# Four cross attentions, one self attention and a routed expert stage of a decoder on one Trainium2 core: first queries copied directly, first maxima placed by a table, rows of maxima moved in the queue, routed counts summed by TensorE

## The chip, the cores and the metric

One program runs on 1 core of one Trainium2 chip. The metric is the device time in microseconds (us), the median of the runs. The engines are TensorE (PE, its weight loads PEld), VectorE (DVE), ScalarE (ACT), GpSimd (POOL) and SyncE (SP), which issues most DMAs. SBUF holds the tiles, PSUM (`ps`) the products of TensorE.

## What is computed

The reference takes x (16, 112, 256) and a context (16, 375, 256), and adds to x, layer by layer, a gated attention and a gated feed-forward part, each on the normalised rows of x:

```
x = x + tanh(g_xattn[0]) * cross_attention_0(LN(x), ctx)
x = x + tanh(g_ffn[0])   * experts_by_position(LN(x))
x = x + tanh(g_xattn[1]) * cross_attention_1(LN(x), ctx)
x = x + tanh(g_ffn[1])   * lora_experts(LN(x))
x = x + tanh(g_xattn[2]) * decoder_block(LN(x), ctx)   # self attention, cross attention, relu layers
x = x + tanh(g_ffn[2])   * product_keys(LN(x))
x = x + tanh(g_xattn[3]) * cross_attention_3(LN(x), ctx, masks)
x = x + tanh(g_ffn[3])   * routed_top2_experts(LN(x))
```

A cross attention has 16 heads of 16 dimensions: q = x Wq + bq, k and v from the context, softmax(q k^T * scale) v, then Wo. The routed layer takes, for each of 16*112 rows, the two best of 8 experts; each expert is a gated layer of 1024 with a normalisation of its own.

## The kernel before

The program is a chain of stages (`chain()`, from L3245). Each stage gives one program to each engine, and `stage` (L182) ends it with a meeting: every engine drains, adds one to a semaphore and waits for all five. The order of the work on each engine is written out by hand; SP's order of DMAs is the order of its one hardware queue. In the profile these stages begin at about: context 0 us, cross 0 at 309, cross 1 at 671, queries of the self attention at 1229, self attention at 1276, cross 2 at 1430, cross 3 at 2177, routed experts at 2438; between them lie the experts by position, the LoRA experts, and the relu and product-key stages.

The context stage makes keys and values of all four cross attentions for all 16 batches and stores them in DRAM (`key_parts`, `values`). So that bf16 products give nearly float32 scores, a float32 number is held as three bf16 parts (high, middle, low: `PARTS` = 3), and six products of parts are summed in one matmul of 96 rows: `Q_PART` = (0, 0, 0, 1, 1, 2) says which part of the queries stands in each sixth of the rows (`spread(j)`, every sixth row), `K_PART` the same of the keys. Two more rows (96 and 97) hold the negative maximum of each query, in two bf16 parts, against rows of ones in the keys.

**A cross stage** (`cross_stage`, L943) treats 16 batches; four batches are a group (`G` = 4 groups, 448 query columns each).
- Queries (`Queries`, L656). TensorE projects (L689): per group two tiles of 128 dimensions, each with two matmuls of 448 columns. ACT makes the high part (L705), DVE the remainder (L719), ACT the middle part (L700), POOL the low part (L729). SP stores each tile with its three parts in DRAM (`query_parts`, `store`, L676), waits until it has landed, and loads it again as six DMAs in the layout of the score matmuls (`load_queries`, L1011). The weights Wq and Wo and two bias rows are loaded by SP at the beginning of the stage (L651, L653), but for cross 0, whose loads end the context stage.
- Maxima. For each batch 8 `pair`s (L1113): two heads' scores, 112 x 375 each, in two of four PSUM banks; DVE takes the negative maxima of a pair (L1269, with masks L1265). After the eighth, DVE clamps (L1278, L1276), TensorE transposes (`maxima`, L1119), DVE splits the row in two parts (L1284, L1286), and SP copies them into rows 96 and 97 of the batch's queries (`rows`, L1021, two DMAs of 3.5 KB). Their arrival is counted in the same semaphore as the batch's values (`at_maxrow`, `load_values`, L1016).
- A `step` of a batch has 12 score tiles (L1129, with a mask matmul L1126 in cross 3), which ACT exponentiates (L1235), and 48 small products with the values (`weigh`, L1139). Between the score tiles of batch b stand the 8 pairs of batch b + 2 (`PAIR_AT`), the transposition of the maxima of b + 1 at k = 2, and the output of b - 1 (L875, L881, L887). All 16 pairs of batches 0 and 1 stand ahead of step 0.

SP's order at the beginning of a cross stage: weights; keys of batch 0 and 1 (six DMAs each, L931; in cross 3 keys of 0 and three masks); store group 0 and wait for it; load its queries; store 1; keys of 2; stores 2 and 3; values of 0; rows of 0; values of 1 and 2; wait for the stores; queries of group 1. In step b: keys of b + 3, rows of b + 1, values of b + 3.

```
1150      q.project(pe)
1151      for b in range(2):
1152          arrived(b, b, turn0)
1153          for p in range(PAIRS):
1154              pair(b, b, p)
1155          if b == 0:
1156              maxima(0, 0)
```

**Self attention.** `query_stage` projects queries and keys (4 tiles a group, weights loaded at its beginning), with the same stores (L676) and reloads for group 0 (L755, L761); it ends when all stores have landed. `self_stage` loads the other groups.

**Routed experts** (`routed_experts_stage`, L2795). Router logits (L943), the two best experts (L1792 to L1807), then both one-hots are added (L3114) and counted: two float32 matmuls, with a lower triangle (L3009, rows ahead in the batch) and with ones (L3010, rows of the batch). DVE adds the counts of the 16 batches one after another (L3121, 16 instructions), derives the blocks of each expert, adds them one after another (L3126, 7 instructions), and finds the expert of each of 21 blocks (L3127 to L3130), by which POOL gathers the weights (L2926). Then each row's place among the blocks: for each of the two choices compares with 43 bounds (L3146), a sum (L3148), a one-hot of the lane, 112 x 2048 (L3150), and three planes of a one-hot of the block (L3153, L3154, L3155). TensorE inverts the table (L3014, 32 matmuls), DVE turns it into indices (L3167 to L3174), and POOL gathers the rows (L2940), which TensorE turns and multiplies (L3039, the main loop). POOL splits the first weights (L2961) before it gathers rows.

## Time and profile before

| | us |
|---|---|
| median of 3 runs | 2940.99 (2938.33 to 2943.34) |
| the profiled execution, its own time | 2937.35 |
| its span, first to last instruction | 2935.6 |
| TensorE busy in the span | 2572.4 (88%), granted clock 0.919 on the mean |
| DVE, ACT, POOL busy | 1801.1 (61%), 1346.3 (46%), 1127.6 (38%) |
| DMA | 361.72 MB, mean 123 GB/s |

Busy time of an engine is a share of the span; the granted clock is a share of 2.4 GHz, with 0.50 and 1.00 its two levels. A stage in which TensorE is busy less than the others shows where it waits; the views by stretch and by time, quoted below, show for whom.

### The profile page before, as it was taken

The page shows a single profiled execution, that of the slowest core. Times are in us where ns is not written, and L with a number is a line of the kernel's source. Part 1 is how long each engine was busy: PE and PEld are TensorE (multiplying, and loading weights), DVE is VectorE, ACT ScalarE, POOL GpSimd, SP SyncE. Part 2 cuts the span into 40 slices and gives each one's busy share as a digit, 9 for nine tenths or more (in the row PEclk, how much of TensorE's full clock was granted, in tenths as well). Part 3 has the DMA queues.
Part 4 walks back from the last instruction along what each step waited for, and adds up shares of the span by engine and source line. Part 5 has one row for each costly group of instructions (what it writes and reads, how often), then busy time and mean ns, then how long its engine had stood idle before and what let it go on. Part 6 is the DMA issues. An engine that isn't in the chain of part 4 may idle for free. (4 is left out here: it accounts for less than half of the span.)

```text
span 2935.6 us, 57244 instructions
## 1 busy us (share of the span) xinstructions
PE 2572.4 (88%) x21432; PEld 2096.7 (71%) x21432; DVE 1801.1 (61%) x3917; ACT 1346.3 (46%) x2698; POOL 1127.6 (38%) x1409
## 2 busy tenths in 40 slices
PE   7999799997997999869699898888868994999995
PEld 7999487883876777636377666666746873999995
DVE  5666587125874343368488437787758874566765
ACT  4454366323663111247466433344433661555663
POOL 3444311003113333247612233554362113677773
PEclk9999699996998999979799999889977995999998
DMA  8888855327550000062466300000027733455663
GB/s 230 243 246 242 235 160 153 119 88 188 164 174 15 1 0 1 31 165 65 121 185 167 119 1 1 1 1 1 1 69 201 181 95 128 189 203 202 214 221 110
DMA packets 153628, 361.72 MB, mean 123 GB/s; under 512 B 26496, under 2 KB 110336, under 8 KB 138160
## 3 DMA queue, kind: packets, MB, share of 16 engines
q1 hardware_dynamic: 141632, 273.03, 33.0%
q0 software_dynamic: 11760, 85.51, 8.2%
q8 instruction: 152, 2.49, 0.4%
q14 instruction: 84, 0.69, 0.1%
HBM read 269.33 MB, written 88.67 MB: 122 GB/s over the span
## 5 line engine op out<-in xcount | busy, mean ns | idle before, releaser
L1235 ACT ACTIVATE arena<-ps 125x448 f32<-125x448 f32 x768 | 404.7, 545 | 325.9 <-PE ps L1129 321.9
L1269 DVE TENSOR_REDUCE arena<-ps 112x2 f32<-112x750 f32 x384 | 348.4, 931 | 82.2 <-PE ps L1113 79.3
L502 POOL TENSOR_SCALAR ln_var<-ln_mv 112x1 f32<-112x1 f32 x160 | 43.0, 269 | 768.1 <-DVE ln_mv L496 763.8
L3039 PE MATMUL ps<-moe_x_r,moe_w_r 128*128 128x256 f32 x2016 | 254.8, 288 | 9.2 <-DVE arena L3199 7.8
L1129 PEld LDWEIGHTS ps<-arena,wreg 98*125 98x125 bf16 x2304 | 215.8, 143 | 60.6 <-issue 18.9
L3039 PEld LDWEIGHTS ps<-moe_x_r,moe_w_r 128*128 128x128 f32 x2016 | 249.1, 195 | 12.0 <-DVE arena L3199 8.8
L1113 PE MATMUL ps<-wreg,arena 96*112 96x375 bf16 x768 | 217.7, 372 | 31.9 <-DMA arena<-query_parts 18.6
L1129 PE MATMUL ps<-arena,wreg 98*125 98x112 bf16 x2304 | 237.3, 228 | 3.7 <-ACT arena L1235 2.9
L1139 PE MATMUL ps<-arena 125*17 125x112 f32 x6144 | 199.2, 263 | 0.6 <-ACT arena L1235 0.6
L428 POOL TENSOR_TENSOR arena<-arena 128x375 bf16<-128x375 f32 x128 | 114.6, 918 | 166.4 <-ACT arena L365 166.4
L285 PE MATMUL ps<-kv_ctx_r,kv_w_r 128*128 128x376 f32 x768 | 145.7, 339 | 21.5 <-DVE kv_w_r L391 14.6
L3084 ACT ACTIVATE arena<-ps,wreg 128x256 f32<-128x256 f32 x168 | 80.1, 477 | 171.4 <-PE ps L3039 152.7
L2961 POOL TENSOR_TENSOR moe_w_r<-wreg,moe_w_r 128x512 fp32r<-128x512 f32 x105 | 139.5, 1355 | 39.7 <-ACT moe_w_r L3067 39.3
L1139 PEld LDWEIGHTS ps<-arena 125*17 125x17 f32 x6144 | 133.4, 98 | 28.6 <-issue 10.8
L285 PE MATMUL ps<-kv_w_r,kv_ctx_r 128*125 128x256 f32 x1152 | 149.5, 282 | 0.0
L3050 PE MATMUL ps<-wreg,arena 128*128 128x256 f32 x672 | 148.5, 380 | 0.0
L285 PEld LDWEIGHTS ps<-kv_ctx_r,kv_w_r 128*128 128x128 f32 x768 | 130.9, 190 | 24.7 <-issue 22.1
L2611 POOL TENSOR_TENSOR arena<-arena 112x1024 f32<-112x1024 f32 x48 | 90.6, 1905 | 149.6 <-DVE arena L2730 138.7
L1265 DVE CUSTOM_DVE_ANT_0 ps<-ps,arena 112x375 f32<-112x375 f32 x256 | 134.2, 573 | 20.0 <-PE ps L1113 17.9
L285 PEld LDWEIGHTS ps<-kv_w_r,kv_ctx_r 128*125 128x125 f32 x1152 | 144.8, 186 | 0.0
L3050 PEld LDWEIGHTS ps<-wreg,arena 128*128 128x128 f32 x672 | 126.4, 191 | 16.0
L399 DVE SCALAR_TENSOR_TENSOR arena<-ps,attn_cols,arena 128x375 f32<-128x375 f32 x128 | 71.9, 604 | 104.1 <-ACT arena L361 103.9
(363 smaller groups left out, 5879.4 us busy)
## 6 DMA issues: line engine op xcount, KB each, us to landing
wreg<-key_parts SPq DMA_DIRECT2D x288, 187.5 KB, 4.0
key_parts<-arena SPq DMA_DIRECT2D x128, 281.2 KB, 4.0
arena<-query_parts SPq DMA_DIRECT2D x108, 224.0 KB, 4.6
values<-arena SPq DMA_DIRECT2D x64, 357.0 KB
arena<-values SPq DMA_DIRECT2D x64, 357.0 KB
arena<-key_parts SPq DMA_DIRECT2D x96, 187.5 KB, 4.0
query_parts<-arena SPq DMA_DIRECT2D x40, 336.0 KB, 5.7
wreg<-in_e_w SPq DMA_DIRECT2D x16, 704.0 KB, 5.3
```

Source lines behind the costliest of these rows:

```text
L285: mm = pe.matmul(dst, lhs(i, c), rhs(j, c), start=(n == 0 and c == 0), stop=(n == len(PRODUCTS) - 1 and c == DC - 1))
L428: pool.tensor_tensor(parts[i % 2][:, t, 2, :], rest[i % 2][:, t, :], parts[i % 2][:, t, 1, :], ALU.subtract).then_inc(part_lo, 1)
L1113: mm = pe.matmul(ps[0:T, 2 * (p % 2) + e, 0:S2], queries(b)[0:SROWS, hd, :], keys[r][0:SROWS, hd, :], start=True, stop=True)
L1129: mm = pe.matmul(ps[0:KN, bank, g * T:(g + 1) * T], keys[r][:, hd, c * KN:(c + 1) * KN], queries(b)[:, hd, :], start=not masked, stop=not ...
L1139: mm = pe.matmul(ps[32 * g:32 * g + VW, SUMS, j * T:(j + 1) * T], vals[r][:, c, 4 * j + g, :], probs[(j * KC + c) % PROBS][:, g * T:(g + 1 ...
L1235: act.activation(probs[k % PROBS], ps[0:KN, 4 + k % 2, 0:GT], ACT.Exp, scale=scale).then_inc(at_probs, 1)
L1265: mm = dve.tensor_tensor_reduce(bank, bank, pen[r], 1.0, 3 * NEG, ALU.add, ALU.max, negmax[r % 2][:, 2 * p + e:2 * p + e + 1])
L1269: dve.tensor_reduce(negmax[r % 2][:, 2 * p:2 * p + 2], ps[0:T, 2 * (p % 2):2 * (p % 2) + 2, 0:S2], AX.X, ALU.max, negate=True).then_inc(at ...
L2611: pool.tensor_tensor(sums[hd], sims[q][:, hd, 0:PI].unsqueeze(2).broadcast_to([T, PI, PK]), sims[q][:, PH + hd, :].unsqueeze(1).broadcast_ ...
L2961: pool.tensor_tensor(w_r[1][:, :, :, cols], w_in[j % 2][:, :, :, cols], w_r[0][:, :, :, cols].bitcast(F32), ALU.subtract).then_inc(m_low, 1)
L3039: mm = pe.matmul(ps[:, f % 4, q * BS:(q + 1) * BS], w_r[wp][:, q, c, f * 128:(f + 1) * 128], x_r[u][xp][:, c, :], start=(n == 0 and c == 0 ...
L3050: mm = pe.matmul(ps[:, 5 + u, q * D:(q + 1) * D], hid[u][:, f, q * 128:(q + 1) * 128], w_out[u][:, f, :], start=(f == 0), stop=(f == FC - 1))
```

## The change

- `Queries.spread_first`: the parts of group 0 are copied from SBUF straight to the layout of the scores, each level as soon as both its tiles are made; no store and no reload of group 0, in the four cross stages (queries) and in the query stage (queries and keys). Columns of Wq are permuted on the host (`by_halves`) so that a partition of the parts holds both tiles of two neighbouring heads; `query_parts` gets rows of 1,792 B. The parts lie as (part, tile), and a store is one DMA per group and kind.
- `QueryWeights` are loaded in the stage before: in the context stage ahead of its last stores, at the beginning of the experts by position, during the self attention, in the product-key stage (Wo of cross 3 in the stage itself). One bias row instead of two, one DMA for each weight.
- A table (`FIRST_PAIRS`, `MAXIMA_AT`): only batch 0's pairs and two of batch 1 stand ahead of step 0; step 0 holds 12 pairs (6 of batch 1, 6 of batch 2), step 1 holds 10 (2 of batch 2, 8 of batch 3). From step 2 on it is as before. The projection of group 3 is cut in four and laid between the pairs of batch 0 (`LAST_GROUP_AT`).
- SP: keys of 0, direct queries, keys of 1, stores 1 and 2, values of 0, rows of 0, keys of 2, values of 1; in step 0 keys of 3, rows of 1, then queries of group 1, values of 2, store of group 3, values of 3. The rows have a semaphore of their own.
- POOL fills each key tile's rows of ones between the low parts of two groups, no longer all behind.
- Routed experts: one-hots, triangle and ones in bf16; the matmul with ones comes first; the counts of earlier batches are added by 15 further matmuls in PSUM; DVE sums over batches in one reduction (`of_expert`) and over experts by a product with a table (`blocks_ahead`) and a reduction. Block and lane come from a rounding (`WHOLE`) for both choices at once; the block's one-hot is one comparison, its second plane DVE's, its first ACT's. Two planes instead of three. POOL waits for the row indices only, not for those of the way back.

```diff
+            def spread_first(self, sp, kind, dest, order, arrived):
+                for level, made in enumerate((part_hi, part_mid, part_lo)):
+                    sp.wait_ge(made, self.q0 + (kind + 1) * DC)
+                    for j, q in enumerate(order):
+                        if q == level:
+                            sp.dma_start(dest[spread(j), :, :].rearrange("d h n -> d (h n)"),
+                                         self.parts[0][:, q, kind * DC:(kind + 1) * DC, :].rearrange("p t n -> p (t n)")).then_inc(arrived, 16)
...
+        LAST_GROUP_AT = {1: (0, 0), 3: (0, 1), 5: (1, 0), 7: (1, 1)}
+        FIRST_PAIRS = ({0: ((1, 2), (1, 3)), 1: ((1, 4),), 2: ((1, 5),), 3: ((1, 6),), 4: ((1, 7),), 6: ((2, 0),), 7: ((2, 1),),
+                        8: ((2, 2),), 9: ((2, 3),), 10: ((2, 4),), 11: ((2, 5),)},
+                       {0: ((2, 6),), 1: ((2, 7),), 3: ((3, 0),), 4: ((3, 1),), 5: ((3, 2),), 6: ((3, 3),), 7: ((3, 4),), 8: ((3, 5),),
+                        9: ((3, 6),), 10: ((3, 7),)})
+        MAXIMA_AT = (6, 3)
...
                 load_keys(sp, keys[0], kv, 0, 0)
-                q.store(sp, 0)
-                q.stored(sp, 0)
-                load_queries(0, range(len(Q_PART)))
-                q.store(sp, 1)
...
+                q.spread_first(sp, 0, group_q[0], Q_PART, group_in[0])
+                weights.load_late(sp)
+                load_keys(sp, keys[1], kv, 1, 1)
+                for g in range(1, G - 1):
+                    q.store(sp, g)
                 load_values(0, 0)
-                rows(0, 0)
+                rows(0)
+                load_keys(sp, keys[2], kv, 2, 2)
+                load_values(1, 1)
...
                     if has(b, 1):
-                        rows(b + 1, place(1))
+                        rows(b + 1)
+                    if b == 0:
+                        q.stored(sp, G - 2)
+                        load_queries(1, range(len(Q_PART)))
+                        load_values(2, 2)
+                        q.store(sp, G - 1, q_last)
...
+                pe.wait_ge(loaded, q.ready)
+                q.project(pe, range(G - 1))
+                arrived(0, 0, turn0)
+                for p in range(PAIRS):
+                    pair(0, 0, p)
+                    if p in LAST_GROUP_AT:
+                        tile, chunk = LAST_GROUP_AT[p]
+                        q.project_tile(pe, G - 1, tile, (chunk,))
+                arrived(1, 1, turn0)
+                pair(1, 1, 0)
+                maxima(0, 0)
+                pair(1, 1, 1)
...
+                    pe.wait_ge(row_in, row_in0 + (n0 + b + 1) * 32)
...
                 for p in range(PAIRS):
                     reduce_pair(0, 0, p)
                 clamp(0, 0)
                 split_rows(0, 0)
+                q.remainders(dve, range(G - 1, G))
...
-                for b in range(B):
-                    link(dve.tensor_tensor(run[:, b + 1, :], run[:, b, :], counts[:, b, :], ALU.add))
+                link(dve.tensor_reduce(of_expert, ps[:, 2, 0:B * E].rearrange("p (b e) -> p e b", e=E), AX.X, ALU.add))
...
-                for e in range(1, E):
-                    link(dve.tensor_tensor(first[:, e:e + 1], first[:, e - 1:e], blocks_of[:, e - 1:e], ALU.add))
+                link(dve.tensor_tensor(blocks_ahead, ahead, blocks_of.unsqueeze(1).broadcast_to([128, E, E]), ALU.mult))
+                link(dve.tensor_reduce(first, blocks_ahead, AX.X, ALU.add))
...
-                pool.wait_ge(m_inverse, INVERTED)
+                pool.wait_ge(m_inverse, INVERTED - 4)
```

## Rows read from the trace of the kernel before

**Rows 1.** Busy time by stretch: us; busy of each engine; PEclk, DMA share, GB/s.

```profile
372.00:500.00 128.00, 125.54 (x2030) 102.55 (x2029) 107.80 (x189) 87.29 (x187) 20.25 (x47) 1.00 0.63 176
671.00:716.00 45.00, 29.19 (x68) 12.04 (x69) 19.89 (x28) 10.45 (x18) 22.47 (x18) 0.65 0.80 223
...
2438.00:2497.00 59.00, 18.50 (x106) 17.25 (x107) 32.54 (x86) 6.57 (x12) 23.37 (x64) 0.50 0.44 161
2497.00:2890.00 393.00, 385.24 (x2663) 367.61 (x2663) 254.72 (x498) 226.97 (x502) 286.46 (x274) 0.99 0.56 197
```

**Rows 2.** Who waited for whom, whole trace, PE: us in total, times, longest us.

```profile
PE ps L689 <- DMA attn_rows<-in_attn_rows: 35.8, 5, 8.1
...
PE ps L1113 <- DMA arena<-query_parts: 18.6, 8, 5.9
```

**Rows 3.** Instructions in order of time, cross 1, from its first DMA on.

```profile
670.71 0.39 SPq L651 DMA_DIRECT2D wlow<-in_attn_w  x1
...
677.91 9.20 PE L689 MATMUL ps<-xn_t,wlow 128*128 128x448 f32 x16 [7.65 <-DMA attn_rows<-in_attn_rows]
...
685.20 2.03 POOL L729 TENSOR_TENSOR arena<-wreg,arena 128x448 bf16<-128x448 f32 x2 [9.32 <-ACT arena L700]
...
700.62 7.51 DVE L1269 TENSOR_REDUCE arena<-ps 112x2 f32<-112x750 f32 x8 [5.44 <-PE ps L1113]
...
709.37 1.17 SPq L1021 DMA_DIRECT2D arena<-arena  x2
...
715.74 0.62 PE L1129 MATMUL ps<-arena,wreg 98*125 98x112 bf16 x4
```

**Rows 4.** DMA issues of cross 0's beginning, 309 to 360 us: KB each, median us to landing.

```profile
DMA packets 5447, 12.11 MB, mean 237 GB/s; under 512 B 949, under 2 KB 4277, under 8 KB 4869
...
arena<-query_parts SPq DMA_DIRECT2D x12, 224.0 KB, 4.7
```

**Rows 5.** In order of time: first instruction of cross 0, 2 and 3; batch 3's transposition in each cross.

```profile
309.66 5.13 POOL L1070 MEMSET wreg<- 2x3000 f32 x2 [4.36 <-SPq L192]
...
374.18 0.26 PE L1119 MATMUL ps<-ident,arena 112*16 112x112 f32 x1
...
739.81 0.26 PE L1119 MATMUL ps<-ident,arena 112*16 112x112 f32 x1
...
1430.30 0.39 SPq L651 DMA_DIRECT2D wlow<-in_attn_w  x1
...
1497.93 0.26 PE L1119 MATMUL ps<-ident,arena 112*16 112x112 f32 x1
...
2177.16 0.39 SPq L651 DMA_DIRECT2D wlow<-in_attn_w  x1
...
2254.33 0.26 PE L1119 MATMUL ps<-ident,arena 112*16 112x112 f32 x1
```

**Rows 6.** Cross 3, in order of time: two pairs; SP's rows of batch 1; step 1's beginning.

```profile
2210.21 1.89 PE L1113 MATMUL ps<-wreg,arena 96*112 96x375 bf16 x4 [0.20 <-DVE arena L1265]
...
2226.20 1.17 SPq L1021 DMA_DIRECT2D arena<-arena  x2
...
2236.88 0.63 PE L1126 MATMUL ps<-unit,arena 112*125 112x448 bf16 x1 [1.81 <-DMA arena<-arena]
```

**Rows 7.** Who SP waited for, 1262 to 1280 us, the end of the query stage.

```profile
SPq L192 <- DMA query_parts<-arena: 6.1, 1, 6.1
```

**Rows 8.** Routed experts before their main loop, in order of time.

```profile
2460.72 3.10 DVE L3121 TENSOR_TENSOR arena<-arena,ps 128x8 f32<-128x8 f32 x16
...
2466.52 0.23 DVE L3130 TENSOR_SCALAR arena<-arena 128x21 uint32<-128x21 f32 x1
...
2469.98 2.30 DVE L3150 TENSOR_TENSOR h<-arena 112x2048 bf16<-112x2048 f32 x1
2472.32 0.86 DVE L3153 TENSOR_TENSOR h<-arena 112x672 bf16<-112x672 f32 x1
...
2489.54 1.41 POOL L2940 DMA_INDIRECT xn_t<-tokens,arena  x1 [5.78 <-DVE arena L3174]
```

More of the change, by code:

```diff
@@ new lines, in store @@
+            def store(self, sp, g, into=None):
+                for kind in range(self.kinds):
+                    sp.wait_ge(part_lo, self.q0 + g * self.tiles + (kind + 1) * DC)
+                    sp.dma_start(query_parts[kind, :, g].rearrange("q p n -> p q n"),
+                                 self.parts[g][:, :, kind * DC:(kind + 1) * DC, :].rearrange("p q t n -> p q (t n)")
+                                 ).then_inc(q_stored if into is None else into, 16)
+            def stored(self, eng, g):
+                eng.wait_ge(q_stored, 16 * (self.st0 + g * self.kinds))
@@ L693, in remainder, with project @@
+            def project(self, pe, some=range(G)):
+                for g in some:
+                    for j in range(self.tiles):
+                        self.project_tile(pe, g, j)
             def remainder(self, n):
@@ new lines, in gpsimd @@
+                for b in range(B):
+                    if b >= 2:
+                        norm.deviation(pool, b - 2)
+                    if masked and has(b, 3):
+                        weighty(b + 3)
+                    if b == 0:
+                        pool.wait_ge(part_lo, q.done)
+                        if masked:
+                            pool.wait_ge(at_pen, p0 + RING)
+                        ones(pool, RING - 1)
+                        pool.wait_ge(const_made, ones_made)
+                        pool.wait_ge(loaded, q.ready)
+                        out.bias.scale(pool)
+                        for ahead in range(BIAS_AHEAD):
+                            out.bias.piece(pool, ahead)
+                    elif b + BIAS_AHEAD - 1 < B:
+                        out.bias.piece(pool, b + BIAS_AHEAD - 1)
+                    if b >= 3 and norm.gain is not None:
+                        norm.keep_scaled(pool, b - 3)
@@ L1107, in tensor @@
+                for b in range(B - 3, B):
+                    if b > B - 3:
+                        norm.deviation(pool, b)
+                    if norm.gain is not None:
+                        norm.keep_scaled(pool, b)
             def tensor(pe):
```

384 lines of the change are left out of this document (208 added, 176 removed).

## The prediction

> **What bounds the kernel now.** The first view is busy time by stretch. In the steady part of a cross stage TensorE is busy 125.5 of 128 us at a granted clock of 1.00, and in the main loop of the routed stage 385 of 393 us [rows 1]: nothing that another engine saves there shortens the program. The 45 us at the beginning of cross 1 are another picture, TensorE busy 29 us at a mean clock of 0.65, and so are the 59 us ahead of the routed main loop, TensorE 18.5 us at 0.50 (1.2 GHz), DVE 32.5 us [rows 1]. The change works on these beginnings. The second view, the waits of the whole trace, says for whom TensorE waits: 35.8 us in five waits for weights and bias rows, and 18.6 us for queries on their way back from DRAM [rows 2]. The third, instructions in time, gives the order of one beginning. Counted from the stage's first DMA at 670.71 (call it s): projection from s+7.2, last low part of group 0 at s+16.5 (the POOL row's end), then its store and reload, first maxima at s+29.9, rows of maxima issued s+38.7, step 0 from s+45.0, although the rows were on their way long before: TensorE's own order puts 16 pairs ahead, each 0.94 us of DVE (7.51/8) [rows 3]. The DMA engines are the fourth: 12.11 MB in 51 us, 237 GB/s, and a query DMA takes 4.7 us to land [rows 4].
>
> **A cross stage after the change, part by part.** I follow it to batch 3's transposition, k = 2 of step 2, from where on the order is the old one. Before, that is 64.5, 69.1, 67.6 and 77.2 us after the first instruction of cross 0 (309.66), 1, 2 and 3 [rows 3, 5].
> - Weights: projection starts at s+0.6 instead of s+7.2 (6 us; in cross 0 its loads, issued before the stage, held it to 314, 4.5 us). SP's three or four DMAs move into the stage before, whose TensorE loop hides them; in cross 0 they move ahead of the last stores of the context stage, 0.5 to 0.65 MB at 237 GB/s [rows 4] are 2 to 2.7 us of transfers that the last stores may now stand behind. Nothing if there is slack, 2.7 us if there is none; I take 1 us lost, once.
> - Direct queries: the low parts of group 0 end 9.3 us after projection starts (677.91 to 687.23) [rows 3], so at s+10. The high and middle copies are then on the way; the last of six lands 3 to 4.7 us later [rows 4], s+13.5. Projection of three groups ends at about the same time (two groups took 9.2 us, partly at the low clock [rows 3]; the third I put at 3 to 4). First pair s+13.5; before, the first maxima, which take one pair of 0.9 us ahead of them, stood at s+29.9.
> - Eight pairs at 0.94 us are 7.5; clamp, transposition, split and issue 1.2 (end of the reductions at 708.13 to 709.37) [rows 3], s+22.2. Group 3's four cuts lie between the pairs, about 0.8 us each at full clock; beside 0.94 us of DVE per pair they fit, at the low clock they cost 1 to 2 us. The two row DMAs: no row shows a small DMA on an idle queue. From above it is cross 3's, issued from 2226.20, for which TensorE waited 1.81 us until 2236.88 [rows 6], 10.7 us with queries, masks and keys ahead; from below the issue itself, 1.2 us. Ahead of them now are at most store 2 and values of 0, 1.1 MB or 4.5 us issued 3 us earlier. I take 4.8: step 0 starts at s+27.
> - Steps 0 and 1 up to the transposition took 24.1 us (715.74 to 739.81) [rows 3, 5]. They get six pairs more (12 and 10 instead of 8 and 8): 5.6 us by DVE's 0.94, 5.7 us by TensorE's 0.95 at the low clock (1.89 for two [rows 6], about half that at full clock). I add 5: 29 us, so s+56.
> - POOL's rows of ones (2.6 us each) now stand between low parts; the low parts of group 2 come at about s+19 for a store that SP can issue before the rows at s+22. SP's queries of group 1 and keys of 3 are needed at s+54 and s+43 and are issued before s+41. I cost these at nothing; the cover is 2 to 3 us at keys of 2, least of all.
> - Sum: 64.5-56 = 8.5, 69.1-56 = 13.1, 67.6-56 = 11.6. Cross 3 waits for one penalty before its pairs (first pair s+15), and a pair costs 1.05 us (1.89 and a wait of 0.20 for two) [rows 6]: rows issued s+24.6, step 0 s+29; step 1 to the transposition took 17.5 us before (2236.88 to 2254.33) [rows 5, 6], step 0, of the same 12 tiles, I put at 13.5 without its wait; with 5 added, s+65 against 77.2: 12.2. **Cross stages together: 45.4 us saved.** All later steps are bound by TensorE [rows 1] and only shift.
>
> **Query stage.** Its end waited 6.1 us for the last stores [rows 7]. It loses a store of 1.3 MB and a read of it from DRAM; with fewer and larger DMAs I take 2.5 us saved, between nothing and 5. Six loads instead of three at its beginning may take back up to 1 us; I take 0.5. The self attention itself keeps its order: 2 us.
>
> **Routed stage.** 16 additions took 3.10 us from 2460.72, the weights' index was ready 2.9 us after them, at 2466.75 [rows 8]; of these 6 us, 23 single additions become a reduction, a product and a reduction of some 0.25 us each (the shortest rows are 0.19 to 0.23) [rows 8], 3.7 us less, and the bf16 products ahead save 0.5 to 1: 4.5 us earlier. From there to the rows' index it was 22.8 us (to 2489.54) [rows 8]. What stays: one-hot of the lane, 2 x 2.30; two comparisons and two planes of 0.86 [rows 8]; 8 small ones of 0.2 to 0.4; inversion of 1.3 to 1.9 us; 5 short ones: 4.6 + 3.5 + 2.4 + 1.9 + 1.3 = 13.7, about 9 less. But POOL splits three tiles of weights before it gathers rows, and I let that cost 2.5 us of the 13.5: **11 us saved** (4.5 if the splits come as late as the weights, 13.5 if they never hold). The main loop starts earlier by this and is otherwise as before.
>
> **The sum**: 45.4 + 2 + 11 - 1 = 57.4 us off the profiled execution's 2937.35, so 2880.0. The median of the runs shown is 3.6 us above that execution: **2884**.
>
> **The rules that speak against it.** Cross 3's rows of batch 1 took 10.7 us behind larger transfers [rows 6]. The Trainium skill ("DMA: Bandwidth & Descriptors", "Queues, rings and completion order") says that each DMA engine consumes its descriptors in ring order. By that rule and this row, two tiny DMAs cost what stands ahead of them, and the change gives them a wait of TensorE's own in every step; it is the mechanism of the slower rival.
> TensorE's clock was at its low level while it worked in short bursts between waits, 0.65 on the mean of cross 1's beginning [rows 1]. The skill ("TensorE: Matmul & The Clock Gate", "HAM oscillation — how this bites in real kernels") ties this to waits for DMA between bursts of matmuls; by it fewer waits would also buy clock, which is a rival below.
>
> **Rivals.**
> 1. *The DMA engines set the beginning* (27%). 12.1 MB went in the first 51 us at 237 GB/s [rows 4]. Nearly the same bytes (less the 0.7 MB of one store) are needed before step 2, and they idle until the first parts are made: 48 + 9 us, step 2 at s+58 to 60 instead of 54. Then each cross saves 5 us less: 20 us lost, 2904. For it: the share of 0.80 over the whole beginning [rows 1]; against: half of it was spent before anything needed it.
> 2. *The clock stays up* (15%). Projection and pairs follow without a gap, and if the wait for rows is short, steps 0 and 1 run at full clock; 12 pairs at 0.94 bound step 0, about 3 us less per cross: 2872.
> 3. *The rows come late in each of steps 0 to 15* (4%). Place: `row_in`, waited for before the first score tile of each step. In the steady part the rows are issued behind keys of b + 3, 1.1 MB or 4.7 us, and TensorE waits only if they come later than a step of 10.7 us; at 3 us of wait a step, 64 steps cost 192 us, at 0.9 us a step the gain of 57.4 is gone. With half of the steps waiting 2 us it is 2884 + 64 = 2948. Against: the same order held before in the steady part with TensorE busy 98% [rows 1].
> 4. *The table does not do what it says* (4%): if step 0 waits for DVE's 12 maxima and again for the split of batch 1, which stands behind them, 10 us of each cross go and about 2924 is left.
>
> **How the numbers follow.** The forecast, at 50%, covers 2873 to 2895: 3 us either way in each cross shift it by 12, cut for independence. Low end 2862: the clock rival with DMA landing at 3 us. High end 2906: the DMA rival, with 8 instead of 11 us in the routed stage. 0.2% is 5.9 us, what a measurement here can tell from no change. Slower by more than that: most of rival 3, 0.03; the same 0.02; faster 0.95.
>
> **What the profile would show.** Waits of the projection for `attn_rows` only in the query stage; no wait of a pair for `query_parts` in group 0; first pair 13 to 15 us after a cross's first DMA; step 0 at s+27; batch 3's transposition at s+56 (s+65 in cross 3); steady steps of 10.7 us; the first gather of rows some 11 us nearer to the routed stage's first logits. A transposition at s+60 or later with a DMA share over 0.9 says rival 1; PEclk over 0.8 there, rival 2; a wait of score tiles for the small DMA in later steps, rival 3. Steady steps that are longer than before would make the prediction wrong altogether.

## The result and the profile after

The changed kernel takes **2910.99 us** (median of five runs, 2908.76 to 2918.49), the kernel before, on the same chip, 2938.33 (2929.93 to 2943.34): ratio 0.9916, 95% interval 0.9892 to 0.9940. Run once more on another chip it gives 0.9918 (0.9903 to 0.9934). It is faster by 27 us (25 by the ratio) where 57 were forecast, and 2911 lies outside the range of 2862 to 2906. Its profiled execution is the slowest of the five: 2918.49 us, span 2916.8.

The chip's trace gives the length of every stage (from the barrier at its beginning to the next), before and after: context 305.2 and 310.0; cross 0 223.7 and 225.2; cross 1 231.4 and 229.7; query stage 47.5 and 46.2; cross 2 230.9 and 233.4; cross 3 260.8 and 253.6; routed stage 497.5 and 483.6. The four cross stages together went from 946.8 to 941.9, so they gave 5 us instead of 45; in the control run (the changed kernel once more, `after2` below) they took 925.7, which is 21 us. Two executions of one kernel differ here by 16 us, so below a time is taken from the ratio, and a trace is read for its order and its waits.

Busy time by stretch, kernel after: a steady part of cross 0, cross 1 up to step 1, the last 16 us before its step 2, the 4 and 7 us ahead of and around cross 0's step 2, the routed stage before its main loop, the main loop. Columns as in [rows 1]; the DMA share can come out a little above 1.

```profile
377.00:505.00 128.00, 123.75 (x1973) 100.62 (x1966) 105.00 (x183) 84.28 (x181) 19.61 (x46) 0.98 0.59 167
677.20:722.90 45.70, 37.45 (x238) 22.39 (x238) 28.31 (x39) 19.01 (x34) 23.56 (x19) 0.77 0.75 193
723.00:738.90 15.90, 9.50 (x143) 6.89 (x136) 9.77 (x17) 5.45 (x12) 0.00 (x0) 0.91 1.02 267
365.00:369.00 4.00, 3.96 (x70) 3.01 (x68) 3.34 (x6) 2.42 (x5) 0.00 (x0) 1.00 1.07 253
369.00:376.30 7.30, 2.56 (x17) 2.22 (x17) 1.36 (x4) 1.09 (x2) 0.00 (x0) 0.63 1.00 235
2432.60:2482.00 49.40, 17.45 (x117) 16.60 (x117) 24.07 (x57) 8.52 (x15) 23.12 (x79) 0.50 0.52 192
2490.00:2870.00 380.00, 377.15 (x2611) 358.91 (x2610) 242.21 (x491) 217.73 (x493) 279.81 (x271) 1.00 0.58 204
```

In cross 1's first 46 us TensorE is now busy 37.5 us where it was 29.2. Then, right before step 2, it is busy 9.5 of 16 us and the DMA engines are full: share 1.02, 267 GB/s. Where the change was to save time, time is lost again. The steady part (123.8 of 128 us) and the main loop (377 of 380) are as full as before.

The waits of PE over the whole trace, kernel after:

```profile
PE ps L1190 <- issue: 21.2, 5, 5.5
...
PE ps L1174 <- DMA arena<-arena: 14.3, 4, 4.0
...
PE ps L718 <- DMA attn_rows<-in_attn_rows: 7.8, 1, 7.8
...
PE ps L1174 <- DMA arena<-query_parts: 7.2, 6, 2.4
```

Against [rows 2]: 35.8 us in five waits for weights are 7.8 in one (the query stage), 18.6 us for queries from DRAM are 7.2 in six short ones. Of the 18.6, three first pairs took 14.4, so the waits in later steps have grown, from 4.2 us to 7.2. New are 14.3 us for the direct queries, once in each cross, and 21.2 us ahead of a score tile (L1190): 15.5 of them before step 2 in crosses 0 to 2, 5.7 before step 0 in crosses 1 and 2. "issue" means that the profile names no releaser; the order in time shows it. Cross 1 of the kernel after, in order of time; SP's rows of maxima are L1072, direct queries L696, queries from DRAM L1062, values L1067, store of a query group L702, keys L985:

```profile
677.65 8.40 PE L718 MATMUL ps<-xn_t,wlow 128*128 128x448 f32 x16 [0.48 <-ACTq L192]
683.53 3.85 SPq L696 DMA_DIRECT2D arena<-arena  x6
...
693.40 1.50 PE L1174 MATMUL ps<-wreg,arena 96*112 96x375 bf16 x4 [3.93 <-DMA arena<-arena]
...
703.92 1.18 SPq L1072 DMA_DIRECT2D arena<-arena  x2
...
706.49 0.65 PE L1190 MATMUL ps<-arena,wreg 98*125 98x112 bf16 x4 [2.87 <-issue]
...
717.16 2.24 SPq L1072 DMA_DIRECT2D arena<-arena  x2
719.44 3.76 SPq L1062 DMA_DIRECT2D arena<-query_parts  x6
723.24 1.02 SPq L1067 DMA_DIRECT2D arena<-values  x2
724.31 0.39 SPq L702 DMA_DIRECT2D query_parts<-wreg  x1
724.75 1.86 SPq L1067 DMA_DIRECT2D arena<-values  x2
726.65 4.54 SPq L985 DMA_DIRECT2D wreg<-key_parts  x6
731.24 1.22 SPq L1072 DMA_DIRECT2D arena<-arena  x2
...
738.92 0.64 PE L1190 MATMUL ps<-arena,wreg 98*125 98x112 bf16 x4 [5.20 <-issue]
...
741.43 0.39 PE L1180 MATMUL ps<-ident,arena 112*16 112x112 f32 x1
```

With s = 677.62, the stage's first DMA: projection at s+0, direct queries issued s+5.9 to s+9.8, first pair s+15.8, rows of batch 0 s+26.3, step 0 s+28.9, rows of batch 1 s+39.5, and then the stall: TensorE idle 5.20 us before step 2, which starts at s+61.3. The two small DMAs that it waits for were issued at 731.24 and 731.87. What L1072's DMAs took to land, first the pair at 703.92, then the pair at 731.24:

```profile
DMA to landing us min/median/max: 1.7/1.8/1.8
...
DMA to landing us min/median/max: 6.2/6.6/7.0
```

731.9 plus 7.0 is 738.9: step 2 starts when the second row lands. The other crosses have the same wait: 4.8 us in cross 0, 5.5 in cross 2; in cross 3, whose steps have 12.7 us, 0.7 us. In the control run it is 4.4, 3.4 and 4.0 us in crosses 0 to 2, and cross 1's step 2 starts at s+55.4.

Batch 3's transposition, from the stage's first DMA, in the four crosses:

```
                                     cross 0   1     2     3
forecast                                56    56    56    65
before                                  64.5  69.1  67.6  77.2
after, profiled execution               61.8  63.8  65.5  70.3
after, control run                      61.2  57.9  61.6  70.1
a_defer (experiment)                    55.8  57.0  59.5  65.7
```

Added over the four crosses, the transposition comes 17 us earlier than before in the profiled execution, 28 in the control run and 40 in a_defer, where 45 were forecast. What lies behind it was to stay as long as it was. By the lengths of the stages it grew: from 668 us before to 681, 675 and 677.

The routed stage before its main loop, kernel after, in order of time:

```profile
2454.49 1.53 PE L3114 MATMUL ps<-arena 112*112 112x120 bf16 x15
...
2454.73 0.29 DVE L3227 TENSOR_REDUCE arena<-ps 128x8 f32<-128x128 f32 x1 [0.55 <-PE ps L3111]
...
2456.88 0.23 DVE L3235 TENSOR_SCALAR arena<-arena 128x21 uint32<-128x21 f32 x1
...
2459.19 2.29 DVE L2969 TENSOR_TENSOR h<-arena 112x2048 bf16<-112x2048 f32 x1
...
2473.27 0.99 POOL L3040 DMA_INDIRECT xn_t<-tokens,arena  x1 [1.04 <-DVE arena L3277]
```

Against [rows 8]: the 16 additions of 3.10 us are gone, TensorE's 15 products that give the running counts take 1.53 us beside VectorE. The stage starts at 2432.64 (before at 2437.58), so the weights' index comes 24.2 us after its beginning instead of 28.9, the first gather of rows 40.6 instead of 52.0.

### The profile page after: what moved, and what is told of

The parts are those of the page before. It is cut to its first block, busy times and chain, and to the rows that moved or that the text cites. A ratio compares the mean times of both kernels' runs of the same rounds, so it can differ in the third digit from the quotient of the medians.

```text
span 2916.8 us, 57251 instructions
## 1 busy us (share of the span) xinstructions
PE 2563.3 (88%) x21445; PEld 2098.6 (72%) x21445; DVE 1783.5 (61%) x3888; ACT 1345.5 (46%) x2700; POOL 1124.9 (39%) x1424
## 4 chain that ended last, share of the span: by engine, by line
PE 59%; DVE 11%; DMA 9%; issue 7%; POOL 6%; ACT 5%; SPq 3%; POOLq 0%; DVEq 0%; ACTq 0%
PE ps L3146 8%; PE ps L1190 6%; PE ps L1200 5%; PE ps L1174 5%; PE ps L3157 5%; DMA key_parts<-arena 4%; PE ps L1745 3%; PE ps L2344 2%; PE ps L928 2%; PE ps L2103 2%; POOL arena L428 2%; PE ps L2337 2%; PE ps L718 2%; PE ps L2093 2%; PE ps L1187 2%
## 5 line engine op out<-in xcount | busy, mean ns | idle before, releaser
L1304 ACT ACTIVATE arena<-ps 125x448 f32<-125x448 f32 x768 | 405.2, 545 | 293.7 <-PE ps L1190 290.2
L1190 PEld LDWEIGHTS ps<-arena,wreg 98*125 98x125 bf16 x2304 | 217.1, 143 | 87.1 <-issue 46.5
L1190 PE MATMUL ps<-arena,wreg 98*125 98x112 bf16 x2304 | 238.5, 229 | 27.9 <-issue 21.2
L1174 PE MATMUL ps<-wreg,arena 96*112 96x375 bf16 x768 | 204.7, 354 | 27.0 <-DMA arena<-arena 14.3
```

The costliest lines, as they stand in the source:

```text
L1174: mm = pe.matmul(ps[0:T, 2 * (p % 2) + e, 0:S2], queries(b)[0:SROWS, hd, :], keys[r][0:SROWS, hd, :], start=True, stop=True)
L1190: mm = pe.matmul(ps[0:KN, bank, g * T:(g + 1) * T], keys[r][:, hd, c * KN:(c + 1) * KN], queries(b)[:, hd, :], start=not masked, stop=not ...
L1304: act.activation(probs[k % PROBS], ps[0:KN, 4 + k % 2, 0:GT], ACT.Exp, scale=scale).then_inc(at_probs, 1)
```

## The experiments

Theory V (volume): before step 2 the DMA engines have more to move than they can, and 1.1 MB of it (the store of query group 3, 672 KB, and the values of batch 3, 398 KB) nobody needs yet. Its rival R: the small rows are late for their own place in SyncE's order. Ratios are to the kernel before, run on the same chip beside each group. The groups are c_ctx, a_defer, b_rows and e_routed; d_table, d_defer, g_keys1 and h_store0; the control run, i_best and j_best_notable; and k_actrows alone. A comparison across groups is one of ratios.

**c_ctx**, the loads of the first weights back behind the last stores:

```diff
-                load_ahead(sp)
                 step(B - 1, 1, None)
+                load_ahead(sp)
```

> The changed kernel with one order put back: the loads of the first cross's weights stand behind the last stores of the context stage again. Theory: those loads (0.65 MB) delayed the last key stores, for whose buffers ScalarE waits, and cost the 4.8 us by which cross 0 starts later (314.4 instead of 309.6). Then cross 0 starts at 309 to 311 again; its projection, which no longer finds the weights there, waits 3 to 5 us as it did before the change (L718 waiting for the weights), so the transposition of batch 3's maxima stays where it was, near 376, and the whole gives 0 to 3 us: the move gained nothing net. Rival 1, the 4.8 us are chance between executions: cross 0 starts at 314 as before the edit, and the program is slower by 3 to 5 us through the wait for weights. Rival 2, the projection's wait is hidden behind the later waits (queries, rows): all 4.8 us come back, ratio to the kernel before about 0.990 against the changed kernel's 0.9916.

Measured: 2908.15 us, ratio 0.9902 (0.9880 to 0.9923), not clear of the changed kernel's 0.9916 and 0.9918. ScalarE's waits for key stores, from 285 us to the end of the stage, in the kernel before, in the changed kernel and in c_ctx:

```profile
ACT arena L361 <- DMA key_parts<-arena: 7.2, 4, 2.5
```

```profile
ACT arena L361 <- DMA key_parts<-arena: 11.1, 5, 4.8
```

```profile
ACT arena L361 <- DMA key_parts<-arena: 8.2, 5, 2.4
```

and c_ctx's first projection:

```profile
315.61 1.83 PE L718 MATMUL ps<-xn_t,wlow 128*128 128x448 f32 x2 [6.35 <-DMA attn_rows<-in_attn_rows]
```

The longest wait doubles with the loads ahead, and the projection's wait goes from 6.35 to 2.84 us. In all eleven traces with the loads ahead, ScalarE's fourth last evacuation (L361) starts 10.5 to 11.9 us after its eighth last, in the three with the old order (before, c_ctx, e_routed) 8.0 to 8.2: 3.1 us lost at the end of the context stage on the mean, 3.5 us gained in cross 0. A gain of the move isn't shown. That the stage itself is 3.1 us longer isn't shown either: on the chip of this group it took 307.8 us in c_ctx, and 307.8 and 310.3 with the loads ahead (a_defer, b_rows). Over all eleven it varies by more, and mostly with the chip: 315.0 to 316.5 us in the four kernels of the group of d_table, where the kernel before is slow as well (2945.8 us against 2928.8 to 2938.3 beside the other runs), 306.8 to 310.3 us in the other seven.

**a_defer**, the store of group 3 and the values of 3 behind the rows of 2:

```diff
                         load_values(2, 2)
+                    if b == 1:
                         q.store(sp, G - 1, q_last)
-                    if has(b, 3):
+                        load_values(3, 3)
+                    if has(b, 3) and b > 0:
                         at_least(sp, at_pv, (n0 + b) * STEPS if has(b, -1) else 0)
...
```

> The changed kernel with two transfers moved on SyncE: the store of query group 3 (0.69 MB) and the values of batch 3 (0.4 MB) go behind the rows of batch 2 in step 1 instead of ahead of the keys of 4. Theory V (volume): in crosses 0 to 2 TensorE waits 4.8 to 5.5 us before step 2, because the DMA engines have at most 240 GB/s and 1.1 MB stand ahead that nobody needs yet. Then the waits shrink by 4 to 4.6 us each, batch 3's transposition comes at s+57 to s+62 instead of s+61.8, 64.2, 66.4, 70.7, and the program is 12 to 18 us shorter than the changed kernel: ratio 0.986 to 0.9875. Theory N (the volume is needed either way, or the deferred bytes come back as a wait in steps 2 and 3): the wait moves one step on, at most 4 us gained, ratio 0.990 to 0.992.

Measured: 2891.52 us, ratio **0.9840** (0.9815 to 0.9866), 23 us less than the changed kernel's 0.9918 gives. SyncE in cross 1 (first DMA at 665.98; rows of 2 at 714.66), and batch 3's transposition:

```profile
704.30 1.16 SPq L1072 DMA_DIRECT2D arena<-arena  x2
705.50 4.31 SPq L1062 DMA_DIRECT2D arena<-query_parts  x6
709.86 1.03 SPq L1067 DMA_DIRECT2D arena<-values  x2
710.93 3.67 SPq L985 DMA_DIRECT2D wreg<-key_parts  x6
714.66 1.21 SPq L1072 DMA_DIRECT2D arena<-arena  x2
715.91 0.59 SPq L702 DMA_DIRECT2D query_parts<-wreg  x1
```

```profile
722.98 0.26 PE L1182 MATMUL ps<-ident,arena 112*16 112x112 f32 x1
```

The same 15.9 us of cross 1 as above (723.0 to 738.9 there), counted from the first DMA:

```profile
711.36:727.26 15.90, 13.90 (x215) 10.45 (x214) 13.41 (x24) 8.24 (x17) 1.76 (x4) 1.00 1.02 267
```

The wait before step 2 is gone in all crosses, and nothing takes its place in steps 2 and 3. The DMA engines are exactly as full, 1.02 and 267 GB/s, yet TensorE is busy 13.9 us instead of 9.5: what changed is which transfers come first. The rows of cross 1 still take 6.0 to 6.2 us to land, but they are issued 4.9 us earlier, counted from the first DMA, and so land before step 2. Theory V holds against N. Its "at most 240 GB/s" was too low: both kernels moved 267. It gained more than its 12 to 18 us. A part, some 3 us, is the step behind the stall: 11.4, 11.4, 11.7 and 13.6 us in the four crosses of the changed kernel, 10.7, 10.7, 11.0 and 12.7 in a_defer. There TensorE's clock is lower: in cross 0 it was 1.00 ahead of the stall and 0.63 on the mean over the 7.3 us around its end (1.2 GHz for a part of them). The rest isn't accounted for.

One rival is not separated. The two transfers also occupy SyncE while it issues them, 2.3 us (724.31 to 726.61), so a_defer takes away bytes and issuing time at once, and no run takes away one of them alone.

**b_rows**, the rows of 2 alone moved ahead of the keys of 4:

```diff
                 def step(b, place, turn):
+                    if b == 1:
+                        rows(b + 1)
                     if has(b, 3):
...
-                    if has(b, 1):
+                    if has(b, 1) and b != 1:
                         rows(b + 1)
```

> The changed kernel with the two small DMAs of batch 2's rows moved ahead of the keys of 4 in step 1; nothing else. Theory V (volume): the rows then land 1 to 4 us earlier, but the keys of 4, that the first pair of step 2 needs, landed only 0.6 us before the rows and still have the same bytes ahead, so the wait moves from the score tile to batch 4's first pair and 0 to 3 us in all are gained: ratio 0.9905 to 0.992. Theory R (rival: the rows' own place in the queue costs the 5 us): the stall before step 2 goes and nothing takes its place, 12 to 16 us gained, ratio 0.986 to 0.988.

Measured: 2902.34 us, ratio 0.9883 (0.9859 to 0.9908). Cross 1, the first pair of batch 4 in step 2:

```profile
734.31 0.84 PE L1176 MATMUL ps<-wreg,arena 96*112 96x375 bf16 x2 [3.65 <-issue]
```

The wait has moved from the score tile to this pair, which needs the keys of 4, as V said: 4.6, 3.7 and 3.2 us in crosses 0 to 2 (13.9 us for L1176 <- issue in all). So R is refuted as the whole cause. The ratio, with an interval that reaches both, lies between V's 0.9905 and R's 0.988: the rows' place may be worth some microseconds of its own, which the next run, where the rows are early as well, did not show.

**k_actrows**, the rows of 2 issued by ScalarE on its own queue:

```diff
-                    if has(b, 1):
+                    if has(b, 1) and b != 1:
                         rows(b + 1)
...
+                        if k == 5 and b == 1:
+                            act.wait_ge(at_mmid, n0 + 3)
+                            for part in range(2):
+                                act.dma_start(queries(2)[SROWS + part:SROWS + part + 1], maxrow[0][:, part, :]).then_inc(row_in, 16)
```

> The changed kernel with the two small DMAs of batch 2's rows issued by ScalarE, in step 1 behind its sixth activation, on a queue of their own; all of SyncE's transfers keep their order. It tells why they took 5.7 and 6.5 us to land in the changed kernel: by the place in the queue (behind SyncE's 2 MB) or by the load of the DMA engines as such. If place (theory P), they land in 1.7 to 3 us, at about s+51, long before step 2; but the keys of 4 keep the bytes ahead of them and land at s+61, so, as in b_rows, TensorE's wait before step 2 moves from the score tile to batch 4's first pair and the gain is that of b_rows, ratio 0.987 to 0.9895. If load (theory L), they land 5 to 7 us after their issue, at s+53 to 55, still before step 2, with the same result for the time; only the landing differs. If ScalarE's issue disturbs its activations: a wait of 1 to 2 us of TensorE for L1304 in step 1, ratio 0.990 to 0.992.

Measured: 2904.57 us, ratio 0.9902 (0.9881 to 0.9923). The two DMAs of cross 0:

```profile
L1316 ACTq DMA_DIRECT2D arena<-arena x2: 609/1086/1562, 357.8 to 358.5; - x2
...
DMA to landing us min/median/max: 5.3/6.3/7.3
```

Not theory P: in a queue of their own all eight took 5.0 to 7.3 us, with 1.7 to 2.0 MB of SyncE's transfers issued and not yet landed (an estimate: each such DMA counted whole). This is the landing that theory L named. TensorE's wait moved to batch 4's first pair (4.3, 3.0, 3.4 us) as in b_rows. The third reading, that ScalarE's issue disturbs its activations, doesn't show: TensorE has no wait of over 0.5 us for L1304 in step 1. The ratio lies just above the 0.9895 that was expected, with an interval that reaches well below it.

**d_table**, the changed kernel without its table, and **d_defer**, a_defer without it:

```diff
-                pair(1, 1, 1)
+                for p in range(1, PAIRS):
+                    pair(1, 1, p)
...
-            if b < len(FIRST_PAIRS):
-                return FIRST_PAIRS[b].get(k, ())
...
-        MAXIMA_AT = (6, 3)
+        MAXIMA_AT = (2, 2)
```

> The changed kernel without the table: all eight pairs of batch 1 before step 0, batches 2 and 3 beside steps 0 and 1 (8 and 8 instead of 12 and 10 pairs), rows of maxima at k = 2 as before. Prediction on record: the table brings 7.5 us (eight pairs of 0.94 us later) less 5 (six pairs more in steps 0 and 1), so 2.5 us per cross, 10 in all: ratio to before 0.995. Theory V (the DMA engines set step 2, not the pairs): what is late before step 2 in the changed kernel is a transfer, so a later step 0 only eats the stall of 5 us; batch 3's transposition stays within 1.5 us of s+61.8 to 70.7, the time within 6 us of the changed kernel, ratio 0.9900 to 0.9935.

Measured: 2906.76 us, ratio 0.9878 (0.9858 to 0.9897), against 0.9918 (0.9903 to 0.9934) of the control run: the changed kernel is faster without its table, by 12 us, and the intervals don't overlap. Cross 0, from its first DMA: batch 3's transposition at 59.0, with the table at 61.2 and 61.8. SyncE's rows of 1 and of 2 and the start of step 2 in d_table (first DMA at 319.89):

```profile
356.53 1.16 SPq L1070 DMA_DIRECT2D arena<-arena  x2
...
369.39 1.22 SPq L1070 DMA_DIRECT2D arena<-arena  x2
...
377.46 0.41 PE L1188 MATMUL ps<-arena,wreg 98*125 98x112 bf16 x4 [1.42 <-issue]
```

and in the changed kernel (first DMA at 314.50):

```profile
352.12 1.16 SPq L1072 DMA_DIRECT2D arena<-arena  x2
...
365.64 2.08 SPq L1072 DMA_DIRECT2D arena<-arena  x2
...
373.75 0.65 PE L1190 MATMUL ps<-arena,wreg 98*125 98x112 bf16 x4 [4.78 <-issue]
```

With the table the rows of 1 are issued at 37.6 instead of 36.6, and everything queued behind that wait of SyncE follows: the rows of 2 at 51.1 instead of 49.5. So the transfers come 1.6 us later, step 2 starts at 59.3 instead of 57.6, and TensorE reaches it early only to wait, with the clock falling (0.63 above). No run moved the transposition alone, so that this delay is the whole loss isn't shown.

> The kernel a_defer (store of group 3 and values of 3 behind the rows of 2) without the table, as d_table. There TensorE has no stall before step 2, so the table's own worth must show: by the prediction's terms 2.5 us per cross, 10 in all, ratio 0.9874 against a_defer's 0.984, batch 3's transposition near s+58.5, 60, 63, 69. Rival: the pairs in steps 0 and 1 are free (VectorE has room beside 12 tiles), then the whole 7.5 us per cross show: 30 us, ratio 0.994. Rival: step 2 of a_defer is still set by transfers: 0 to 1 us per cross, 0.984 to 0.9855.

Measured: 2906.34 us, ratio 0.9852 (0.9829 to 0.9874) against a_defer's 0.9840 (0.9815 to 0.9866): the table now brings 3.5 us at the middle, but the intervals overlap widely. The 30 us are ruled out; neither 10 us nor nothing is. Transposition at 60.6, 58.3, 57.4 and 67.1.

**e_routed**, the kernel before with the routed stage of the change alone (its hunks from `before`, `ones`, `both` on):

> The kernel before with the routed stage of the change alone (bf16 products of counts, prefix by TensorE, shorter chain on VectorE). Prediction on record: 11 us saved, ratio 0.9963. From the trace of the changed kernel, in which the routed stage is 13.9 us shorter than before (483.6 against 497.5): ratio 0.9953. If part of these 13.9 comes from elsewhere (POOL or DMA engines freed by the other parts), less: 0.997.

Measured: 2927.51 us (12 runs), ratio 0.9964 (0.9947 to 0.9981), or 10.6 us: the forecast of 11. The routed stage was 489.4 us in this trace and 483.5 to 489.4 in the other twelve with the new code, so the 483.6 of the profiled execution was a short one, and its 13.9 us less than before overstate the gain.

**g_keys1**, a_defer with the keys of 1 behind the store of group 1:

```diff
-                load_keys(sp, keys[1], kv, 1, 1)
-                for g in range(1, G - 1):
+                q.store(sp, 1)
+                load_keys(sp, keys[1], kv, 1, 1)
+                for g in range(2, G - 1):
                     q.store(sp, g)
```

> The kernel a_defer with the keys of batch 1 behind the store of query group 1 (so issued at about s+15.6 instead of s+10.2). In the changed kernel the last of the six direct query DMAs of cross 1 landed 6.6 us after its issue, at s+16.1, where 3 to 4.7 were forecast; the keys of 1 (1.1 MB) were issued right behind it. If they share the DMA engines with the queries (theory S), the first pair comes 1 to 1.6 us earlier, at s+14.5 to 15.1; batch 1's first pair then waits 0 to 2 us for its keys at s+24, and the total changes by -4 to +4 us: ratio 0.9825 to 0.9855. If the queries' landing is their own length (six times 0.23 MB in small rows, theory L), the first pair stays at s+15 to 16.2, and the total is the same or up to 6 us longer: ratio 0.984 to 0.986.

Measured: 2897.55 us, ratio 0.9841 (0.9825 to 0.9858). The first pair of cross 1 now waits 2.37 us for its queries, not 3.9, and starts 13.8 us after the first DMA:

```profile
688.47 0.85 PE L1177 MATMUL ps<-wreg,arena 96*112 96x375 bf16 x4 [2.37 <-DMA arena<-arena]
```

This looks like theory S, but other traces speak against most of it. With the keys of 1 in their old place, cross 1's first pair waited 3.9 us in three kernels (the changed one, a_defer, d_defer) and 2.5 to 2.7 us in five (the control run, c_ctx, b_rows, d_table, k_actrows), and started at s+14.0 to 14.6 in those. Against them the new place gives 0.2 to 0.3 us. Long waits, of 3.5 us or more, are found in 9 of the 32 first pairs with the keys in the old place and in 1 of 12 with the new one, so the keys may make them more frequent; that isn't shown. The trace's cross stages sum to 905.3 us against a_defer's 915.0, but the ratio is the same; a gain is not shown.

**h_store0**, a_defer without direct queries in the crosses:

```diff
...
-                q.spread_first(sp, 0, group_q[0], Q_PART, group_in[0])
+                q.store(sp, 0)
+                q.stored(sp, 0)
+                load_queries(0, range(len(Q_PART)))
```

> The kernel a_defer without the direct queries in the cross stages: group 0 is stored to DRAM (one DMA), the store awaited, and read back by six DMAs. By the prediction's terms the last low part of group 0 is at s+10, the store takes 4.7 us or more to land, the read back 3.8 us of issue and 4.7 of landing: first pair at s+23 to 25 instead of 15 to 16, everything behind it 7 to 9 us later per cross, 28 to 36 in all: ratio 0.994 to 0.996. Rival (the later transfers set step 2 anyway, volume 1.4 MB more, or the start is partly hidden): only 2 to 5 us per cross, ratio 0.987 to 0.991.

Measured: 2916.79 us, ratio 0.9909 (0.9893 to 0.9925): the direct queries are worth 0.0069, 20 us, or 5 per cross. The first pair of cross 1 starts 19.7 us after the first DMA, 4.4 us later than in a_defer:

```profile
697.58 1.50 PE L1178 MATMUL ps<-wreg,arena 96*112 96x375 bf16 x4 [8.30 <-DMA arena<-query_parts]
```

In the four crosses it starts 4.3 to 5.5 us later. The ratio is the rival's (0.987 to 0.991), but not by its mechanism: there is no long wait before step 2 that would hide the loss. The way through DRAM is shorter than the forecast's terms made it, by 3 to 5 us (first pair at s+19.7 where s+23 to 25 was expected).

**after2**, the changed kernel unedited:

> The changed kernel itself once more, unedited, beside the two below. Theory T (the table costs more than it brings where 1.1 MB stand too early): the kernel without the table gave 0.9878 and this one 0.9916 on another chip, so here it gives 0.990 to 0.993 again. If that difference was one between chips or executions: 0.987 to 0.989.

Measured: 2908.26 us, ratio 0.9918 (0.9903 to 0.9934). The changed kernel gives the same ratio on two chips, so a difference between chips is an unlikely reason for d_table's 0.9878; the two weren't run on one chip.

**i_best**, g_keys1 with the later query loads ahead of the rows, and **j_best_notable**, the same without the table:

```diff
...
                         load_keys(sp, keys[place(3)], kv, b + 3, place(3))
+                    if GB <= b < B - GB and b % GB < 2:
+                        if b // GB + 1 == G - 1:
+                            q.stored_last(sp)
+                        load_queries(b // GB + 1, range(b % GB * 3, b % GB * 3 + 3))
                     if has(b, 1):
                         rows(b + 1)
...
```

> The kernel g_keys1 (store of group 3 and values of 3 behind the rows of 2; keys of 1 behind the store of group 1), and in steps 4, 5, 8 and 9 the three query loads ahead of the rows of maxima instead of behind the values of b + 3. Both kernels, before and changed, wait 0.5 to 2.6 us for the queries of the next group at two places of each cross, and the step there takes 12 to 14 us instead of 10.7. Theory Q: the loads stand behind two waits of SyncE (for the rows and for the weighting) and are late for that; ahead of them, these waits go: 1 to 2 us at eight places, 8 to 12 us, ratio 0.980 to 0.982 against g_keys1's 0.9841. Rival (bytes: a step that loads keys, values and half a query group has 2.2 MB in 10.7 us anyway): the wait stays or moves to the next rows, ratio 0.983 to 0.985.

Measured: 2877.38 us (2873.80 to 2884.78), ratio **0.9818** (0.9801 to 0.9835), the best of all: by the ratios 53 us under the kernel before and 29 under the changed one, which ran on the same chip (the control run). Against g_keys1 it is 7 us, and the ratio is in theory Q's range, though the intervals overlap. The waits for queries from DRAM at L1177 are gone from the list, the steps at these places are 10.7 to 11.3 us, and the cross stages sum to 899.7 us. What lies behind batch 3's transposition is back to 667 us over the four crosses, where the kernel before had 668.

> The kernel i_best without the table (all eight pairs of batch 1 before step 0, rows of maxima at k = 2). The same pair as d_defer and a_defer (0.9852 and 0.984), with fewer transfers in the way at the beginning: if the table is worth the 2.5 us per cross of the prediction once no transfer is late, this is 10 us slower than i_best, ratio higher by 0.0034; if its worth is bound by the stalls that stay at the first pairs, 0 to 5 us, 0 to 0.0017.

Measured: 2885.21 us, ratio 0.9838 (0.9822 to 0.9854): here the table is worth 0.0020, 6 us, though the intervals overlap and nothing is not ruled out.

## Why the prediction was wrong, and where it was right

- **The step that failed**: "SP's queries of group 1 and keys of 3 are needed at s+54 and s+43 and are issued before s+41. I cost these at nothing". The queries of group 1 were issued from s+41.8, the keys of 4 from s+49.0, the rows of 2 at s+53.6, and between them stood 1.1 MB that step 2 doesn't need. The prediction listed when each transfer is needed, but added up no bytes between s+40 and s+56. There it would have found queries 1.38 MB, values 0.41 twice, a store of 0.69 and keys of 1.15, 4 MB or 17 us at its own 237 GB/s, in 16 us. a_defer puts the price at 0.0078, 23 us, of the 30 by which the gain fell short: with that order the transposition comes at 55.8, 57.0, 59.5 and 65.7, where 56, 56, 56 and 65 were forecast, and 2891.5 is inside the range.
- **A second step that failed**: "All later steps are bound by TensorE [rows 1] and only shift." What lies behind the transposition took 668 us before, 681 in the profiled execution, 675 in the control run and 677 in a_defer. In the changed kernel some 3 us of this are the step behind the stall. More are steps that wait for the next group's queries: 12 to 14 us instead of 10.7 at two places of a cross. The rows of the kernel before had such waits already (4.2 of the 18.6 us in [rows 2]; e_routed, with the old cross stages, has some 672 us there); i_best takes them away and comes to 667. The loss is about the size of the 7 us that a_defer leaves missing.
- **The rival that came true** is the first, the DMA engines, with 27%: step 2 at s+61.3 where it said 58 to 60 (s+55.4 in the control run), DMA share 1.02 where it named 0.9. It took the volume as fixed by the need and so gave 2904; a_defer has the same share and no stall, so it was mostly a matter of order. A full share alone doesn't tell.
- **Rival 3's mechanism** appeared before step 2 of each cross, not in steps 0 to 15; steady steps stayed at 10.7 us. The rule that it cited, ring order ("DMA: Bandwidth & Descriptors", "Queues, rings and completion order" of the Trainium skill), did not decide it: on another queue the rows took 5.0 to 7.3 us all the same.
- **The table** was a term of 2.5 us gained per cross. On the changed kernel it lost 3 us per cross (0.9918 against 0.9878); by the order in the trace the rows of 1, moved to k = 6, hold up SyncE. With the order of a_defer it brought 0.9 us per cross, with that of i_best 1.5, neither clear of nothing.
- **First pair**: s+15.8 instead of s+13.5 in cross 1, s+14.1 in the control run. **Pairs of batch 0** with group 3's cuts: 10.5 us up to the issue of the rows, 8.7 taken. **Small DMAs**: 4.8 us taken, 2.6 from issue to step 0, of which 1.7 to 1.8 is landing. The first two errors made the rows late (s+26.3 instead of s+22.2), and by luck the third took back half: step 0 came at s+28.9 instead of s+27.
- **Context stage**: 1 us lost taken, 3.1 measured at ScalarE's last evacuations, beyond the bound of 2.7; what the early weights gave cross 0 was 3.5, not 4.5.
- **Right**: waits for weights gone but one; steps 0 and 1 up to the transposition (29 us forecast, 28.3 and 29.4 in crosses 0 and 1 of a_defer); the query stage 47.5 to between 44.4 and 46.2 in the twelve traces with its new code (2 us forecast); the routed stage, 10.6 us against 11, with the weights' index 4.7 us earlier (4.5 forecast) and the rows' gather 11.3 us earlier. Within this 11 two terms cancelled: the chain between the two indices gave 6.6 us instead of 9, and POOL's splits took nothing instead of 2.5.
- The clock rival did not come: 0.77 in cross 1's first 46 us where it was 0.65, and low again after the stall. The range's high end adds up to 2907 (2904 and 3), not 2906; nothing hangs on it.

What stays open: whether the stall came from the bytes or in part from SyncE's time to issue them, why the context stage is some 7 us longer on one chip, and whether g_keys1's order and the table are a gain.

## What to carry to other kernels

When a change takes waits out of a beginning, add up, per window between two deadlines, the bytes that its DMA queue holds ahead of each deadline, and the time that issuing them takes, not only the time at which each transfer is issued; what is needed later goes behind the deadline, even if the queue seems free earlier. In a queue that is issued in order, a wait for a computed thing (here the rows of 1) sets the time of everything behind it, so a step that delays the computation also delays transfers that have nothing to do with it. Work that is laid out so that an engine arrives earlier is worth something only if the transfers that it then needs are there. And a wait that appears in one trace and goes in the next is checked in other traces of the same code before it is put down to an edit: cross 1's first wait was 2.5 or 3.9 us with nothing changed there.

## What the runs showed of the hardware

A DMA of one 3.5 KB row took 1.7 to 1.8 us to land when the DMA engines had nothing else to do (cross 1 of the changed kernel, before step 0; share 0.00 over the 2.3 us ahead of it), and 5.0 to 7.3 us on ScalarE's own queue with 1.7 to 2.0 MB issued and not yet landed; on SyncE's queue, at the same point of the changed kernel, it took 5.7 to 7.5 us. For latency a second queue was here no way around the load of the engines. Why, the runs don't tell. The DMA engines moved 267 GB/s over 15.9 us at a share of 1.02, with loads from DRAM and a store mixed; the prediction's 237 was no ceiling.
